# The gate's power on GpSimd for all tiles, and the first tile turned between the matmuls of the third output projection

## The chip, the cores and the metric

The kernel runs on one core of a Trainium2 chip. Its engines work side by side and meet only at semaphores: TensorE (PE in the profile) multiplies matrices, VectorE (DVE) and ScalarE (ACT) work on rows, GpSimd (POOL) takes elementwise work on data in SBUF, and SyncE (SP) issues transfers. The metric is the device time of one execution in microseconds; less is better.

## The reference

One layer of a small transformer in float32, over 4 batches of 256 tokens of width 512 (1024 tokens, 8 tiles of 128):

```
x = x + layernorm(attention(layernorm(x)))        # 32 heads of 16, 8 key/value heads, rotary, causal
x = x + layernorm(ffn(layernorm(x)))
ffn(x):  result = x @ W_base.T + b_base
         probs = softmax(x @ W_gate.T)            # 8 experts
         top two, renormalised: route_w
         delta = sum over experts of (x @ A.T * route_w) @ B.T
         return result + delta
```

Renormalising the top two of a softmax needs only the difference of their two logits: with l1 the largest and l2 the second, the second weight over the first is e^(l2 - l1), and the weights are 1/(1 + that) and that/(1 + that). This one number per token is "the gate's power" of the title.

## The kernel before, in words

The program is written out by hand, one instruction stream per engine; there is no scheduler. Each `wait_ge` is a wait on a semaphore, and each engine works strictly in the order of its stream. After the projections, attention runs over 32 units in a software pipeline of `STEPS` steps. Behind it comes the part that the change touches: a pipeline over the 8 tiles of 128 tokens, `tile_step(s)`, which each engine has in a form of its own. In step s tile s is in the output projection, tile s-1 gets its first residual and the norm ahead of the feed-forward part, tile s-2 is transposed and multiplied with the concatenated weights (base, down projection, gate), tile s-3 is gated and goes through the up projection, tile s-4 gets bias and statistics, and tile s-5 its last norm and residual. Steps 0 and 1 are interleaved with the end of attention (`EARLY`), steps 2 to 12 follow it.

What each engine does in step s, in its order:

- TensorE: `turn_mid(s-2)` (L1188, four transposes), `project_out(s)` (L1179, 12 matmuls: four with the high parts of weight and attention, four with the low part of the weight, four with the low part of attention), `base_down_router(s-2)` in three terms (L1204, 8 matmuls each), with `turn_hw(s-3)` (L1215, one transpose of the gated down projection) behind the first term, and `up_projection(s-3)` (L1219, L1221). Step 2 alone is the other way round: `project_out(2)` first, then waits for the last exponentials and the last copies of attention's output, then `turn_mid(0)`.
- ScalarE: in steps 3 and 4 the gate's power (L678: Exp with scale -1 and the largest logit as bias) and then a one-element square root that brings that function's table back (`bring_table(1, ..)`, L582); `high_of_transpose(s-2)` (L664); square roots of variances (L588); the first residual's norm (L651); the copy of the turned gated tile (L697). At the end of steps 2 and 3 a one-element Exp brings the exponential's table. `attn_high_part` (L658) follows steps 2 and 4.
- VectorE: `gating_choice(s-3)` (L881 the eight largest logits, L883 their indices, L884, L885 the one-hot of the first), `add_bias(s-4)` (L912, L913), statistics of tile s-1 (L777, L778), `gating_weights(s-3)` (L892, L893, L896, L897 make the weights from the power; L901 multiplies the down projection with them), statistics of the output projection of tile s (L777), the low part of the transposed tile s-2 (L937), and the scales and norms (L783, L786, L791).
- GpSimd: from step 5 on `gate_power(s-3)`, then the last residual of tile s-5 (L531) and the first residual of tile s (L536). `attn_low_part` (L513) stands at the end of step 2 and inside step 5, `divide(3)` (L507) at the end of step 3. `gate_power` is a subtraction and a power, both of 128 x 1:

```
pool.wait_ge(top_ready, t + 1)
pool.tensor_tensor(ga[:, 18:19], ga[:, 9:10], ga[:, 8:9], ALU.subtract).then_inc(logit_left, 1)
pool.wait_ge(logit_left, t - POWER_TILE + 1)
pool.tensor_tensor(ga[:, 1:2], e_sb[:, :], ga[:, 18:19], ALU.pow).then_inc(gexp_ready, 1)
```

VectorE's L892 waits for `gexp_ready`. TensorE's `turn_hw` waits for `hw_ready`, which L901 gives; its first term of tile t waits for `xn1_high` (L664) and, from tile 2 on, for `y_ready` of tile t-2 (L913).

Of the kernel before, what the change touches and what calls it, by code (L numbers as in the profile page):

```python
# [65 lines left out]

VECTOR_ATTN = {UNITS: 0, UNITS + 4: 1}
SPREADS = {21: (0,), 25: (1,), UNITS + 1: (2, 3), 37: (4,), 41: (5,), 45: (6,), 49: (7,)}
POWER_TILE = 2


ROPE_3 = {0: 1, 1: 2}
# [11 lines left out]
def build(nc, x, wq, wk, wv, wo, wcat, lora_b, bias, tables, ident, maskq, iota, out):  # L84
    ctx = ExitStack()
    with ctx:
# [360 lines left out]
        def _(pool):  # L447
# [68 lines left out]
            def gate_power(t):  # L516

                ga = gate[:, t % 2, :]
                pool.wait_ge(top_ready, t + 1)
                pool.tensor_tensor(ga[:, 18:19], ga[:, 9:10], ga[:, 8:9], ALU.subtract).then_inc(logit_left, 1)  # L520
                pool.wait_ge(logit_left, t - POWER_TILE + 1)
                pool.tensor_tensor(ga[:, 1:2], e_sb[:, :], ga[:, 18:19], ALU.pow).then_inc(gexp_ready, 1)

            def residuals(s):
# [35 lines left out]
                    pool.tensor_tensor(low, whole, high.bitcast(F32), ALU.subtract).then_inc(weight_low, 1)  # L560
            divide(BATCH - 2)
            for s in range(2, TILES + 5):
                if POWER_TILE <= s - 3 < TILES - 1:
                    gate_power(s - 3)
                if s == TILES + 1:
                    gate_power(TILES - 1)
                if s == 5:
                    attn_low_part(BATCH - 1)
                residuals(s)
                if s == 3:  # L570
                    divide(BATCH - 1)
                if s == 2:
                    attn_low_part(BATCH - 2)
# [3 lines left out]
        def _(act):  # L577
            act.wait_ge(pool_const, 1)

            def bring_table(k, t):  # L580

                nc.scalar.activation(unused[:, k, t:t + 1], eps_sb[:, 0:1], (ACT.Exp, ACT.Sqrt)[k])  # L582
# [90 lines left out]

            def tile_step(s):
                t1, t2, t3, t4, t5 = (s - lag for lag in range(1, 6))
                if 0 <= t3 < POWER_TILE:
                    act.wait_ge(top_ready, t3 + 1)
                    nc.scalar.activation(gate[:, t3 % 2, 1:2], gate[:, t3 % 2, 8:9], ACT.Exp, scale=-1.0,  # L678
                                         bias=gate[:, t3 % 2, 9:10]).then_inc(gexp_ready, 1)
                    bring_table(1, t3)  # L680
                if 0 <= t2 < TILES:
                    high_of_transpose(t2)
                if s < TILES:
# [15 lines left out]
                    output_norm(t5)  # L699
                if 0 <= t4 < TILES:  # L700
                    sqrt(3, t4)
                if 0 <= t2 < POWER_TILE:
                    bring_table(0, t2)

            for n in range(STEPS):
                u = n - ST_LAG
# [302 lines left out]
        def _(pe):  # L1009
# [150 lines left out]
                if kt == qt:  # L1160
                    last.then_inc(o_psum, 1)

            def project_out(t):
                if t == 0:

                    pe.wait_ge(weight_low, 8)
                    pe.wait_ge(s12_free, UNITS)
                if t == 1:

                    pe.wait_ge(mrow_ready, GROUPS)  # L1170
                pe.wait_ge(attn_low, t // 2 + 1)
                if t >= 2:
                    pe.wait_ge(z1_ready, t - 1)
                b = t // 2
                terms = [(attn, w, r) for attn, w in ((attn_h[:, b % 2, :], wo_h), (attn_h[:, b % 2, :], wo_l),
                                                      (attn_l[:, b, :], wo_h)) for r in range(REP)]
                for i, (attn, w, r) in enumerate(terms):
                    col = r * SEQ + (t % 2) * P
                    last = nc.tensor.matmul(ps[:, (t + 1) % 2, :], attn[:, col:col + P], w[:, r, :],  # L1179
                                            start=(i == 0), stop=(i == len(terms) - 1))  # L1180
                last.then_inc(wo_psum, 1)

            def turn_mid(t):
                pe.wait_ge(xn1_ready, t + 1)
# [39 lines left out]
            def tile_step(s):  # L1224
                t2, t3 = s - 2, s - 3
                if s == 2:

                    project_out(s)

                    pe.wait_ge(exp_done, 2 * UNITS)  # L1230
                    wait_o(pe, 2 * GROUPS)
                if 0 <= t2 < TILES:
                    turn_mid(t2)
                if 3 <= s < TILES:
                    project_out(s)
# [83 lines left out]
```

## Time and profile before

| | |
|---|---|
| median of 3 runs | 234.10 us (232.86 to 234.14) |
| the profiled execution's own time | 233.25 us |
| its span, first to last instruction | 231.5 us |
| PE busy | 202.0 us (87%) |
| DVE busy | 173.6 us (75%) |
| ACT busy | 116.8 us (50%) |
| POOL busy | 115.4 us (50%) |
| granted TensorE clock, mean | 0.991 of full speed |

A busy share is an average over the whole span. What a change in one stage is worth is read from that stage: which engine waits there, and what ends its wait last. The tile pipeline's steps 2 to 12 fill the stretch from about 159 us to the end.

### The profile page before, as it was taken

The page shows a single profiled execution, that of the slowest core. Times are in us where ns is not written, and L with a number is a line of the kernel's source. Part 1 is how long each engine was busy: PE and PEld are TensorE (multiplying, and loading weights), DVE is VectorE, ACT ScalarE, POOL GpSimd, SP SyncE. Part 2 cuts the span into 40 slices and gives each one's busy share as a digit, 9 for nine tenths or more (in the row PEclk, how much of TensorE's full clock was granted, in tenths as well). Part 3 has the DMA queues.
Part 4 walks back from the last instruction along what each step waited for, and adds up shares of the span by engine and source line. Part 5 has one row for each costly group of instructions (what it writes and reads, how often), then busy time and mean ns, then how long its engine had stood idle before and what let it go on. Part 6 is the DMA issues. An engine that isn't in the chain of part 4 may idle for free.

```text
span 231.5 us, 3767 instructions
## 1 busy us (share of the span) xinstructions
PE 202.0 (87%) x1304; PEld 122.8 (53%) x1304; DVE 173.6 (75%) x364; ACT 116.8 (50%) x207; POOL 115.4 (50%) x102
## 2 busy tenths in 40 slices
PE   0599999998878979999999989899889989997860
PEld 0484834444444444444444424145778878996840
DVE  1882616867998896859696885685898898898885
ACT  3340531243124877878766785773578335343231
POOL 8200333553357795797743446462756275323352
PEclk9999999999999999999999999999999999999996
DMA  5998049977985102795762203354230000110113
GB/s 166 381 363 338 3 136 204 256 201 167 193 206 144 38 1 72 185 193 103 171 118 65 49 11 51 96 96 96 47 98 0 3 19 26 47 48 0 45 45 136
DMA packets 22465, 26.73 MB, mean 115 GB/s; under 512 B 3760, under 2 KB 17328, under 8 KB 21680
## 3 DMA queue, kind: packets, MB, share of 16 engines
q1 hardware_dynamic: 22304, 26.38, 44.8%
q8 instruction: 10, 0.16, 0.3%
q10 hardware_dynamic: 144, 0.13, 0.2%
q14 instruction: 7, 0.06, 0.1%
HBM read 17.19 MB, written 6.95 MB: 104 GB/s over the span
## 4 chain that ended last, share of the span: by engine, by line
PE 44%; DVE 29%; issue 9%; ACT 8%; DMA 5%; SPq 3%; POOL 1%; DVEq 0%; ACTq 0%; POOLq 0%
PE ps L1046 10%; DVE stats L777 5%; PE ps L1141 5%; PE ps L1156 5%; PE ps L1056 4%; PE ps L1204 4%; DVE nmax L977 3%; PE ps L1115 3%; PE ps L1032 3%; DMA region_b<-q_scr 3%; DVE nmax L974 2%; PE ps L1095 2%; ACT region_a L724 2%; PE ps L1110 2%; DMA x_sb<-x 2%
## 5 line engine op out<-in xcount | busy, mean ns | idle before, releaser
L544 POOL TENSOR_SCALAR_AFFINE_SELECT region_a<-region_a 128x1024 f32<-128x1024 f32 x32 | 36.9, 1153 | 27.4 <-ACT region_a L724 27.1
L977 DVE TENSOR_REDUCE nmax<-ps 128x4 f32<-128x1024 f32 x32 | 39.1, 1222 | 10.3 <-PE ps L1115 10.0
L724 ACT ACTIVATE region_a<-ps 128x1024 f32<-128x1024 f32 x32 | 32.7, 1022 | 0.2 <-PE ps L1141 0.2
L1046 PE MATMUL ps<-region_a,region_c 128*128 128x512 f32 x64 | 29.0, 598 | 0.0
L1141 PE MATMUL ps<-region_b,kst 98*128 98x512 bf16 x96 | 26.9, 381 | 1.6 <-ACT region_a L724 1.1
L721 ACT ACTIVATE region_a<-ps 128x512 f32<-128x512 f32 x32 | 19.2, 599 | 16.9 <-PE ps L1141 16.2
L974 DVE TENSOR_REDUCE nmax<-ps 128x4 f32<-128x512 f32 x32 | 21.8, 682 | 5.1 <-PE ps L1099 4.7
L1156 PE MATMUL ps<-region_a,v_aug 128*32 128x512 f32 x192 | 25.3, 603 | 0.0
L588 ACT ACTIVATE std<-mv,eps_sb 128x1 f32<-128x1 f32 x32 | 9.4, 294 | 29.7 <-DVE mv L778 29.7
L536 POOL TENSOR_TENSOR x_sb<-x_sb,region_b 128x512 f32<-128x512 f32 x8 | 10.2, 1276 | 24.8 <-ACT region_b L651 24.8
L463 POOL TENSOR_TENSOR region_a<-region_a 128x512 f32<-128x512 f32 x4 | 6.5, 1627 | 27.6 <-DVE region_a L825 27.6
L1115 PEld LDWEIGHTS ps<-kst,region_b 96*128 96x128 bf16 x256 | 17.0, 97 | 5.5
L1115 PE MATMUL ps<-kst,region_b 96*128 96x128 bf16 x256 | 19.5, 219 | 0.0
L1046 PEld LDWEIGHTS ps<-region_a,region_c 128*128 128x128 f32 x64 | 11.6, 190 | 12.8 <-issue 12.8
L825 DVE TENSOR_TENSOR region_a<-ps,region_c 128x512 f32<-128x512 f32 x16 | 9.9, 683 | 10.3 <-PE ps L1032 5.5
L1095 PE MATMUL ps<-mask_bf,ident_bf 128*128 128x512 bf16 x32 | 12.3, 385 | 4.2 <-DVE nmax L974 2.1
L777 DVE BATCH_NORM_STATS2 stats<-x_sb 128x6 f32<-128x512 f32 x16 | 11.0, 686 | 6.6 <-DMA x_sb<-x 5.6
L1110 PE MATMUL ps<-mask_bf,ident_bf 128*128 128x512 bf16 x32 | 12.3, 385 | 2.6 <-DVE nmax L977 2.4
L1204 PE MATMUL ps<-wcat_h,xn_h 128*128 128x324 f32 x64 | 11.6, 321 | 3.0 <-ACT xn_h L664 1.9
L1141 PEld LDWEIGHTS ps<-region_b,kst 98*128 98x128 bf16 x96 | 7.6, 97 | 12.3 <-ACT region_a L724 3.4
L611 ACT CAST region_c<-region_a 128x512 bf16<-128x512 f32 x8 | 4.7, 618 | 18.1 <-DVE region_a L833 17.1
L531 POOL TENSOR_TENSOR region_b<-x_sb,region_b 128x512 f32<-128x512 f32 x7 | 9.0, 1280 | 8.9 <-ACT region_b L651 8.8
(107 smaller groups left out, 413.9 us busy)
## 6 DMA issues: line engine op xcount, KB each, us to landing
q_scr<-region_c SPq DMA_DIRECT2D x24, 128.0 KB, 2.6
region_b<-q_scr SPq DMA_DIRECT2D x8, 384.0 KB, 4.9
x_sb<-x SPq DMA_DIRECT2D x8, 256.0 KB, 5.8
region_b<-q_scr SPq DMA_DIRECT2D x8, 256.0 KB, 5.6
attn_t<-o_sb SPq DMA_DIRECT2D x32, 64.0 KB, 2.3
rden_bc<-r_scr SPq DMA_DIRECT2D x8, 256.0 KB, 3.4
out<-region_b SPq DMA_DIRECT2D x7, 256.0 KB, 2.0
kst<-k_scr SPq DMA_DIRECT2D x8, 192.0 KB, 3.1
```

What stands on the lines that cost most here:

```text
L544: pool.affine_select(out=blocks, in_=blocks, compare_op=ALU.is_ge, fill=0.0, base=0, pattern=[[0, 2], [0, REP], [1, P]], channel_multiplie ...
L721: nc.scalar.activation(probs[:, u % PRING, 0, :], ps[:, 3, :], ACT.Exp, scale=float(HEAD_DIM) ** -0.5).then_inc(exp_done, 1)
L724: nc.scalar.activation(probs[:, u % PRING, 1:3, :], ps[:, 4:6, :], ACT.Exp, scale=float(HEAD_DIM) ** -0.5).then_inc(exp_done, 1)
L777: link(nc.vector.bn_stats(stats[:, k, t, :], src))
L974: nc.vector.tensor_reduce(nmax[:, gi % 2, 0, heads], ps[:, 0, :].rearrange("p (r k) -> p r k", r=REP), AX.X, ALU.max, negate=True).then_in ...
L977: nc.vector.tensor_reduce(nmax[:, gi % 2, 1, heads], ps[:, 1:3, :].rearrange("p a (r k) -> p r a k", r=REP), AX.XY, ALU.max, negate=True). ...
L1046: last = nc.tensor.matmul(ps[:, SET_BANKS[i][ri], :], wq_sb[:, c, col:col + P], xn_t[:, c, half * HALF:(half + 1) * HALF], start=(c == 0), ...
L1095: nc.tensor.matmul(ps[:, 0, :], ident_bf[:, :], mask_bf[:, :, :].rearrange("p r k -> p (r k)"), start=True, stop=False, skip_group_check=True)
L1115: last = nc.tensor.matmul(ps[:, 1 + kt, r * P:(r + 1) * P], qst[0:SROWS, slot, h, P:2 * P], kst[0:SROWS, slot, k, kt * P:(kt + 1) * P], st ...
L1141: last = nc.tensor.matmul(ps[:, 3 + j, :], kst[0:TROWS, slot, k, kt * P:(kt + 1) * P], qst[0:TROWS, slot, k * REP:(k + 1) * REP, qt * P:(q ...
L1156: last = nc.tensor.matmul(ps[32 * j:32 * j + 32, 6 + qt, :], v_aug[:, 2 * b + kt, g * GROUP_KV + j, :], probs[:, u % PRING, qt + kt, :], s ...
L1204: last = nc.tensor.matmul(ps[:, 4 + 2 * (t % 2) + hf, 0:CATH], act_part[:, t % 2, c, :], w[:, c, hf * CATH:(hf + 1) * CATH], start=(term = ...
```

## The change

`POWER_TILE` is gone. GpSimd takes the gate's power for tiles 0 and 1 too: `gate_power(0)` stands behind `residuals(2)` and ahead of `attn_low_part(2)`, `gate_power(1)` behind `residuals(3)` and ahead of `divide(3)`. ScalarE loses its two exponentials of the gate and the four one-element activations, with the four loads of a table that they cause. On TensorE `project_out(2)` is cut in two: its first 8 matmuls, then `turn_mid(0)`, then its last 4, and only then the waits for the last exponentials and copies.

```diff
--- before.py
+++ after.py
@@ -66,7 +66,6 @@
 
 VECTOR_ATTN = {UNITS: 0, UNITS + 4: 1}
 SPREADS = {21: (0,), 25: (1,), UNITS + 1: (2, 3), 37: (4,), 41: (5,), 45: (6,), 49: (7,)}
-POWER_TILE = 2
 
 
 ROPE_3 = {0: 1, 1: 2}
@@ -518,7 +517,7 @@
                 ga = gate[:, t % 2, :]
                 pool.wait_ge(top_ready, t + 1)
                 pool.tensor_tensor(ga[:, 18:19], ga[:, 9:10], ga[:, 8:9], ALU.subtract).then_inc(logit_left, 1)
-                pool.wait_ge(logit_left, t - POWER_TILE + 1)
+                pool.wait_ge(logit_left, t + 1)
                 pool.tensor_tensor(ga[:, 1:2], e_sb[:, :], ga[:, 18:19], ALU.pow).then_inc(gexp_ready, 1)
 
             def residuals(s):
@@ -560,13 +559,15 @@
                     pool.tensor_tensor(low, whole, high.bitcast(F32), ALU.subtract).then_inc(weight_low, 1)
             divide(BATCH - 2)
             for s in range(2, TILES + 5):
-                if POWER_TILE <= s - 3 < TILES - 1:
+                if 2 <= s - 3 < TILES - 1:
                     gate_power(s - 3)
                 if s == TILES + 1:
                     gate_power(TILES - 1)
                 if s == 5:
                     attn_low_part(BATCH - 1)
                 residuals(s)
+                if s in (2, 3):
+                    gate_power(s - 2)
                 if s == 3:
                     divide(BATCH - 1)
                 if s == 2:
@@ -673,11 +674,6 @@
 
             def tile_step(s):
                 t1, t2, t3, t4, t5 = (s - lag for lag in range(1, 6))
-                if 0 <= t3 < POWER_TILE:
-                    act.wait_ge(top_ready, t3 + 1)
-                    nc.scalar.activation(gate[:, t3 % 2, 1:2], gate[:, t3 % 2, 8:9], ACT.Exp, scale=-1.0,
-                                         bias=gate[:, t3 % 2, 9:10]).then_inc(gexp_ready, 1)
-                    bring_table(1, t3)
                 if 0 <= t2 < TILES:
                     high_of_transpose(t2)
                 if s < TILES:
@@ -699,8 +695,6 @@
                     output_norm(t5)
                 if 0 <= t4 < TILES:
                     sqrt(3, t4)
-                if 0 <= t2 < POWER_TILE:
-                    bring_table(0, t2)
 
             for n in range(STEPS):
                 u = n - ST_LAG
@@ -1160,7 +1154,7 @@
                 if kt == qt:
                     last.then_inc(o_psum, 1)
 
-            def project_out(t):
+            def project_out(t, first=0, end=3 * REP):
                 if t == 0:
 
                     pe.wait_ge(weight_low, 8)
@@ -1174,11 +1168,13 @@
                 b = t // 2
                 terms = [(attn, w, r) for attn, w in ((attn_h[:, b % 2, :], wo_h), (attn_h[:, b % 2, :], wo_l),
                                                       (attn_l[:, b, :], wo_h)) for r in range(REP)]
-                for i, (attn, w, r) in enumerate(terms):
+                for i in range(first, end):
+                    attn, w, r = terms[i]
                     col = r * SEQ + (t % 2) * P
                     last = nc.tensor.matmul(ps[:, (t + 1) % 2, :], attn[:, col:col + P], w[:, r, :],
                                             start=(i == 0), stop=(i == len(terms) - 1))
-                last.then_inc(wo_psum, 1)
+                if end == len(terms):
+                    last.then_inc(wo_psum, 1)
 
             def turn_mid(t):
                 pe.wait_ge(xn1_ready, t + 1)
@@ -1225,11 +1221,13 @@
                 t2, t3 = s - 2, s - 3
                 if s == 2:
 
-                    project_out(s)
+                    project_out(s, 0, 2 * REP)
+                    turn_mid(t2)
+                    project_out(s, 2 * REP)
 
                     pe.wait_ge(exp_done, 2 * UNITS)
                     wait_o(pe, 2 * GROUPS)
-                if 0 <= t2 < TILES:
+                elif t2 < TILES:
                     turn_mid(t2)
                 if 3 <= s < TILES:
                     project_out(s)
```

GpSimd's stream from the residual of step 2 to that of step 4. L536 (first residual), L513 (low part of attention) and L507 (division) of the kernel before are L535, L512 and L506 of the changed one; L519 and L521 are the subtraction and the power. Before:

```order
L536 TENSOR_TENSOR x_sb<-x_sb,region_b 128x512 [waits z1_ready]
L513 TENSOR_TENSOR attn_l<-attn_t,attn_h 128x1024 [waits attn_low,attn_high]
L536 TENSOR_TENSOR x_sb<-x_sb,region_b 128x512 [waits z1_ready]
L507 TENSOR_TENSOR attn_t<-attn_t,rden_bc 128x1024 [waits num_loaded3,rden_loaded3,rden_loaded2,num_loaded2]
L536 TENSOR_TENSOR x_sb<-x_sb,region_b 128x512 [waits z1_ready]
```

After:

```order
L535 TENSOR_TENSOR x_sb<-x_sb,region_b 128x512 [waits z1_ready]
L519 TENSOR_TENSOR gate<-gate 128x1 [waits top_ready]
L521 TENSOR_TENSOR gate<-e_sb,gate 128x1 [waits logit_left]
L512 TENSOR_TENSOR attn_l<-attn_t,attn_h 128x1024 [waits attn_low,attn_high]
L535 TENSOR_TENSOR x_sb<-x_sb,region_b 128x512 [waits z1_ready]
L519 TENSOR_TENSOR gate<-gate 128x1 [waits top_ready]
L521 TENSOR_TENSOR gate<-e_sb,gate 128x1 [waits logit_left]
L506 TENSOR_TENSOR attn_t<-attn_t,rden_bc 128x1024 [waits num_loaded3,rden_loaded3,rden_loaded2,num_loaded2]
L535 TENSOR_TENSOR x_sb<-x_sb,region_b 128x512 [waits z1_ready]
```

Two pairs of small instructions came in, each between a residual and one of the two long instructions over 1024 columns.

TensorE's stream in step 2, from the second four matmuls of the third output projection to the first term of tile 0 (L1179, L1188, L1204 are L1174, L1184, L1200 in the changed kernel). Before:

```order
L1179 MATMUL ps<-wo_l,attn_h 128x512 x4
L1179 MATMUL ps<-wo_h,attn_l 128x512 x4
L1188 MATMUL ps<-ident_sb,region_b 128x128 [waits xn1_ready,o_ready_vector,exp_done]
L1188 MATMUL ps<-ident_sb,region_b 128x128 x3
L1204 MATMUL ps<-wcat_h,xn_h 128x324 [waits xn1_high]
```

After:

```order
L1174 MATMUL ps<-wo_l,attn_h 128x512 x4
L1184 MATMUL ps<-ident_sb,region_b 128x128 [waits xn1_ready]
L1184 MATMUL ps<-ident_sb,region_b 128x128 x3
L1174 MATMUL ps<-wo_h,attn_l 128x512 [waits z1_ready,attn_low]
L1174 MATMUL ps<-wo_h,attn_l 128x512 x3
L1200 MATMUL ps<-wcat_h,xn_h 128x324 [waits xn1_high,o_ready_vector,exp_done]
```

The four transposes moved ahead of the last four matmuls, and the waits for the copies and exponentials moved from the transposes to the first term. The other engines' streams differ only on ScalarE, by the ten instructions named above that are gone.

## Rows read from the trace of the kernel before

**Rows 1.** Busy time of each engine, one stretch per tile step, s = 3, 4, 6 and following
```profile
core 0: us, PE busy (x) PEld busy (x) DVE busy (x) ACT busy (x) POOL busy (x), PEclk, DMA share, GB/s
167.90:176.54 8.64, 8.05 (x48) 6.97 (x46) 7.24 (x23) 6.43 (x12) 4.24 (x3) 1.00 0.25 65
...
176.54:185.01 8.47, 8.28 (x48) 6.91 (x46) 7.83 (x21) 4.53 (x12) 3.52 (x3) 1.00 0.01 2
...
193.88:201.65 7.77, 7.77 (x47) 7.05 (x45) 7.00 (x27) 3.12 (x7) 3.43 (x5) 1.00 0.09 35
```

**Rows 2.** The chain that ended last, in order of time: start us, us, what
```profile
176.67 2.32 DVE gate L885
...
212.33 0.36 DVE region_b L901
```

**Rows 3.** Timeline, step s = 2: start us, us, engine, line, op, operands, [idle before]
```profile
160.58 1.09 PE L1179 MATMUL ps<-wo_l,attn_h 128*128 128x512 f32 x4
...
161.68 0.55 DVE L791 TENSOR_SCALAR region_b<-x_sb,mv,rstd 128x512 f32<-128x512 f32 x1
...
162.93 0.63 PE L1188 MATMUL ps<-ident_sb,region_b 128*128 128x128 f32 x4 [0.33 <-DVE o_sb L286]
...
164.23 1.45 PE L1204 MATMUL ps<-wcat_h,xn_h 128*128 128x324 f32 x8 [0.68 <-ACT xn_h L664]
...
164.66 0.67 DVE L777 BATCH_NORM_STATS2 stats<-ps 128x6 f32<-128x512 f32 x1
```

**Rows 4.** Timeline, step s = 3
```profile
167.27 1.28 POOL L536 TENSOR_TENSOR x_sb<-x_sb,region_b 128x512 f32<-128x512 f32 x1 [1.20 <-ACT region_b L651]
...
168.10 0.17 DVE L881 MAX8 gate<-ps 128x8 f32<-128x8 f32 x1 [0.49 <-PE ps L1204]
...
169.72 2.38 POOL L513 TENSOR_TENSOR attn_l<-attn_t,attn_h 128x1024 fp32r<-128x1024 f32 x1 [1.17 <-ACT attn_h L658]
...
169.86 1.28 ACT L582 ACT_TABLE_LOAD   x1
...
169.94 2.18 DVE L893 TENSOR_SCALAR gate<-iota_sb,gate 128x8 f32<-128x8 f32 x1
...
171.88 1.47 PE L1204 MATMUL ps<-wcat_h,xn_h 128*128 128x324 f32 x8 [0.59 <-ACT xn_h L664]
...
172.43 0.35 DVE L901 SCALAR_TENSOR_TENSOR region_b<-ps,gate 128x128 f32<-128x128 f32 x1
```

**Rows 5.** Timeline, step s = 4
```profile
175.33 1.27 POOL L536 TENSOR_TENSOR x_sb<-x_sb,region_b 128x512 f32<-128x512 f32 x1 [3.23 <-ACT region_b L651]
...
176.36 0.27 DVE L884 CAST gate<-gate_i 128x2 f32<-128x2 uint32 x1
...
176.56 2.40 POOL L507 TENSOR_TENSOR attn_t<-attn_t,rden_bc 128x1024 f32<-128x1024 f32 x1
...
176.67 2.32 DVE L885 TENSOR_SCALAR gate<-iota_sb,gate 128x8 f32<-128x8 f32 x1
...
180.99 0.35 DVE L901 SCALAR_TENSOR_TENSOR region_b<-ps,gate 128x128 f32<-128x128 f32 x1
```

**Rows 6.** Timeline, step s = 5, where GpSimd already takes the power
```profile
185.38 0.19 POOL L520 TENSOR_TENSOR gate<-gate 128x1 f32<-128x1 f32 x1 [0.19 <-DVE gate L881]
...
185.65 0.55 POOL L522 TENSOR_TENSOR gate<-e_sb,gate 128x1 f32<-128x1 f32 x1
...
185.81 0.23 DVE L885 TENSOR_SCALAR gate<-iota_sb,gate 128x8 f32<-128x8 f32 x1
...
186.17 2.40 POOL L513 TENSOR_TENSOR attn_l<-attn_t,attn_h 128x1024 fp32r<-128x1024 f32 x1
...
187.47 1.12 DVE L893 TENSOR_SCALAR gate<-iota_sb,gate 128x8 f32<-128x8 f32 x1
...
188.53 1.28 POOL L531 TENSOR_TENSOR region_b<-x_sb,region_b 128x512 f32<-128x512 f32 x1
```

**Rows 7.** Line L885 over the whole run: shortest, median and longest, first and last start
```profile
L885 DVE TENSOR_SCALAR gate<-iota_sb,gate x8: 229/231/2320, 168.8 to 220.2; 128x8 f32<-128x8 f32 x8
```

## The prediction

> **What bounds the kernel now.** I read the stretch of the tile steps first, one window per step from one turn of a tile to the next [rows 1]. The reader should compare the lengths: steps 3 and 4 take 8.64 and 8.47 us, step 6 takes 7.77 us with as many matmuls, and in step 6 TensorE is busy for all of its 7.77. So an undisturbed step is bound by TensorE (with VectorE at 7.00 us not far behind), and steps 3 and 4 hold 0.87 + 0.70 = 1.57 us above that, which is most of what this change can reach. In both of them VectorE is busier than in step 6 (7.24 and 7.83) although it does no more work: something makes its instructions long.
>
> The chain of waits says where [rows 2]: it runs through VectorE's L885 at 176.67 for the whole of that instruction's 2.32 us, and it is still on VectorE at 212.33. Apart from its waits for ScalarE's small square roots, the chain does not leave VectorE between these two. Hence a time won on VectorE at the end of step 4 moves all that follows, and time won on TensorE or ScalarE alone does not.
>
> The timelines of the steps name the cause. L885 works on 8 columns; its median over the run is 231 ns, its longest 2320 [rows 7]. The long one starts at 176.67, 0.11 us behind the start of GpSimd's division over 1024 columns (L507, 176.56 for 2.40, end 178.96), and ends at 178.99 [rows 5]. In step 3 the same happens to L893, from 169.94 to 172.12, beside L513, which ends at 172.10 [rows 4]. VectorE's small instructions of this kind are held until a long GpSimd instruction ends. The question for each step is thus which VectorE instruction meets the long one of GpSimd, and when that one starts.
>
> **Step 2: the turn moved into the projection.** Before, the second four matmuls end at 160.58 + 1.09 = 161.67, the last four at 162.60; TensorE is idle for 0.33 us until 162.93 (a copy of attention's output) and for another 0.68 between the turn and the first term at 164.23 [rows 3]. Now the turn needs only the norm of L791, which ends at 161.68 + 0.55 = 162.23. TensorE waits from 161.67 to about 162.3, turns for 0.63 until 162.9, and the last four matmuls cover ScalarE's copy of the turned tile and end at 164.0, where the first term starts: 0.2 us earlier than 164.23. The gain is so small because the idle 1.01 us becomes one of 0.63 plus nothing, and the start stamps overlap. What is put late is the third output projection, by 1.4 us (162.60 to 164.0). VectorE asks for it at 164.66 (L777), so 0.66 us of cover stays. Bounds: if the turn began no sooner than before (162.93), the matmuls would end at 162.93 + 0.63 + 1.09 = 164.65, still inside the cover, and the gain would be below zero by 0.4 on TensorE; at best it is the whole idle second. I take 0.2. The other waits moved behind the last matmuls are over by then: the copy that ended the idle 0.33 is done at 162.9.
>
> **Step 3: the power of tile 0.** Removed from ScalarE: two exponentials and four one-element activations, each of these with a table load of 1.28 us ahead of it [rows 4]: some 5 us of loads over both steps. On TensorE they cost what is seen at 171.88, 0.59 us of waiting for the copy of turned tile 1 [rows 4]; now that copy can run as soon as the tile is turned, beside the output projection. TensorE's gain would be 0.2 + 0.59 = 0.8 us there, but the next thing that it needs is `turn_hw(0)`, behind VectorE's L901, so what counts is VectorE.
>
> VectorE: L881 comes 0.2 us earlier, at 167.9, and the largest logits are ready at about 168.05. GpSimd is in L536 until 168.55 [rows 4]. Behind it come the two new instructions. Their price is in step 5: the subtraction starts at 185.38, the power 0.27 later at 185.65 for 0.55, and L513 follows without a gap (0.52 after the power's start) [rows 6]. Together 0.79 us. So the power starts at 168.8, L513 at 168.55 + 0.79 = 169.34 and, after 2.38, it ends at 171.72 instead of 172.10. (It can start then: ScalarE no longer loads a table ahead of the high part that it needs.) L893 needs the power, which is ready just as L513 begins, so it is held again, until 171.72 instead of 172.12. From there to the end of L901 is 172.78 - 172.12 = 0.66 [rows 4]: 172.4 instead of 172.78, a gain of 0.38 us. It carries over to the first residual of tile 3 (L536 at 175.33 becomes 174.95).
>
> **Step 4: the power of tile 1.** Now the two small instructions stand between L536 and the division. L536 ends at 176.60 - 0.38 = 176.22; the division starts 0.79 later, at 177.0, and ends at 179.4 (before 178.96). VectorE gets its logits 0.4 us earlier; L884 (before at 176.36) starts at about 175.95, L885 at about 176.2 to 176.3. That is behind L536 and ahead of the division, with only the subtraction and the power beside it. Does the power hold it? In step 5 L885 ran at 185.81, inside the power of 185.65 to 186.20, in 0.23 us [rows 6], which is the median of its eight executions [rows 7]. So I take 0.23. From L885's start to L893's it took 187.47 - 185.81 = 1.66 us in step 5 [rows 6], with the same instructions between; so L893 asks at 177.9 to 178.0, finds the division running and is held until 179.4. L901 ends 0.66 later, at 180.1, against 180.99 + 0.35 = 181.34 [rows 5]. Gain on VectorE, and so on all that follows: 1.25 us. Bounds of this term: 1.25 + 0.84 where L893 is not held; 0.4 us lost where L885 still is (rivals below). TensorE can follow: at 7.77 a step instead of 8.64 and 8.47 [rows 1] its own gain by the end of step 4 is up to 0.2 + 1.57 = 1.8 us.
>
> **From step 5 on** I cost nothing: GpSimd has the power there already, every engine starts from VectorE's result, and the holds of step 5 (L893 for 1.12, at L513's end [rows 6]) keep their distance. Work of the added instructions on GpSimd itself, 1.5 us, is hidden: it was busy for 4.24 of 8.64 and 3.52 of 8.47 us in these steps [rows 1].
>
> **The sum.** The profiled execution took 233.25 us, a span of 231.5 and 1.75 around it. 233.25 - 1.25 = 232.0 us. That execution lies 0.85 under the median of the runs (234.10), so the same gain seen from the median would be 232.85; the range has to hold that.
>
> **Rivals.**
>
> *GpSimd's row closes (slower).* The new instructions hold L885 as the long ones do, or it comes too late, and the division begins before it got through. For it: each of the three long instructions of GpSimd in steps 3 to 5 catches a small one of VectorE [rows 4 to 6], and L884 at 176.36 took 0.27. Against: L885 beside the power in rows 6, and that a held instruction does get in where two long ones follow each other: L893 ended at 188.59 although L531 had begun at 188.53 [rows 6]. Price: if only tile 1 is caught, L885 ends at 179.4 instead of 178.99, and the time is 233.25 + 0.4 = 233.7. If tile 0's L885 is caught as well, behind L536 and until 171.7, the work behind it up to L901, 1.7 us (from L885's end at 178.99 to 181.34, less 0.66 for a bias that step 3 has not), ends at 173.4 instead of 172.78; this 0.6 is carried to step 4, where L507 again ends 0.8 behind its old distance: about 234.7. It decides from the point where L885 asks later than the power's end, 0.7 us later than I put it in step 4. The Trainium skill has a rule on this side: "GPSIMD Engine Reference", section "Key points", says that GpSimd shares its SBUF interfaces with VectorE and that VectorE's two-port modes and instructions with two SBUF inputs contend with it, without regard to the length of the GpSimd instruction. By that rule L885 would wait for the subtraction and the power as well, and this rival would be the forecast; the trace agrees for the long instructions (2.32 us), and not for the power (0.23 us in it).
>
> *No hold in step 4 (faster).* L893 escapes the division, because that one starts later (its transfers, or ScalarE) or L893 earlier. Then L901 ends at about 179.0 and TensorE becomes the bound: 233.25 - 1.8 = 231.5; with the hold of step 5 (1.12 - 0.28 = 0.84) gone too, 230.6. Against it: the division has 2.4 us and L893 falls into its middle.
>
> *The gain does not reach the end (no change).* VectorE's lead is lost again in steps 5 to 7, where a last residual of GpSimd may catch an instruction that it let pass before; one such hold is worth 0.8 us: 232.8, two of them 233.25 or above. Against it: all engines start step 5 with the same shift.
>
> **How the numbers follow.** Forecast 0.52 (its own range 231.5 to 232.6, from 0.4 us of uncertainty in where the holds end), slower rival 0.15, faster rival 0.15, no change 0.18. A difference of 1% is 2.3 us, about what a measurement of this kernel can tell from none. The forecast, the no-change case and the slower rival at 233.7 are all within it; the faster rival passes it only where both holds go (230.6), and I allow for holds that I did not see: 0.09 for faster. The slower rival at 234.7 stays within 1%; only more holds of that kind would pass it: 0.04. The range takes in the faster rival down to 231.0, the runs' scatter, and the slower rival's first form: 231.0 to 233.9.
>
> **What would show each step right or wrong.** Right: no table load behind 160 us; the first term of tile 0 at about 164.0 with no wait ahead of it; no wait for ScalarE's copy ahead of tile 1's first term; L893 of tile 0 long and ending at about 171.7; L885 of tile 1 at 0.23 and L893 of tile 1 long, ending with the division at about 179.4; steps 3 and 4 near 8.4 and 7.8 us, step 5 as before. Wrong: an L885 of 2 us or more in step 3 or 4 (slower rival), an L893 of 0.28 us in step 4 (faster rival), or a step from 5 on that is longer than its counterpart before (no change). The forecast fails altogether if statistics of tile 2's output projection wait for TensorE, the cover of 0.66 us being gone.

## The result and the profile after

| | before | changed |
|---|---|---|
| median of 20 runs each | 233.62 us | 232.31 us |
| lowest to highest | 232.24 to 234.72 | 230.92 to 233.46 |
| the profiled execution's own time | 233.25 us | 232.62 us |
| its span | 231.5 us | 230.9 us |

The ratio of changed to before is 0.9947, with a 95% interval of 0.993 to 0.9964: 1.2 us faster, clear of no change but under 1%. (With 20 runs of each kernel the interval is about 0.4 us to either side: a difference of 0.5% can be told from none, where the prediction had put the limit at about 1%.) The two profiled executions differ by 0.63 us only. The rest is not the change's: in the changed kernel's profile everything is already 0.61 us late when the stretch in question begins; most of that is there from the start, where the first loads came later (VectorE's statistics of tile 1 wait for their load until 7.03 us, before until 6.50). A fixed distance is therefore used below, from the start of VectorE's norm of tile 0 in step 2 (161.68 before [rows 3], 162.29 now) to the start of tile 7's turn: 54.46 us before, 53.18 after, 1.28 less. Of these, 0.39 us lie before the turn of tile 1, 0.10 in step 3, 0.71 in step 4 and 0.07 in step 5; the first two are best read together (see e1).

The step windows of the changed kernel, as in [rows 1] (now the third to the sixth window, steps 3, 4, 5 and 6):

```profile
core 0: us, PE busy (x) PEld busy (x) DVE busy (x) ACT busy (x) POOL busy (x), PEclk, DMA share, GB/s
168.12:176.66 8.54, 8.17 (x47) 7.02 (x45) 7.46 (x24) 2.74 (x6) 5.24 (x5) 1.00 0.30 71
176.66:184.42 7.76, 7.76 (x48) 7.04 (x46) 7.08 (x22) 2.68 (x7) 4.44 (x5) 1.00 0.01 2
184.42:193.22 8.80, 8.19 (x47) 7.02 (x45) 8.09 (x25) 3.75 (x8) 5.55 (x6) 1.00 0.08 30
193.22:200.98 7.76, 7.76 (x48) 7.03 (x46) 6.98 (x27) 3.12 (x7) 3.42 (x5) 1.00 0.09 35
```

Step 4 fell from 8.47 to 7.76 us, the length of an undisturbed one; TensorE is busy for all of it. Step 3 (8.54, before 8.64) and step 5 (8.80) still hold about 0.8 and 1.0 us above that. ScalarE's busy time fell from 6.43 and 4.53 us to 2.74 and 2.68, far more than the steps did.

The chain that ended last, in order of time (start, duration, what), against [rows 2]:

```profile
170.34 2.04 DVE gate L887
...
178.64 1.39 DVE gate L887
...
186.88 1.05 DVE gate L887
188.03 1.15 DVE gate L891
```

The 2.32 us of L885 in step 4 are gone from it, but VectorE's L887 (the old L893) is on it for 2.04, 1.39 and, in step 5, 1.05 us, and L891 (the old L897) for 1.15.

Step 2 in the timeline, against [rows 3]; L1184 is the turn, L1174 the projection, L1200 the first term:

```profile
162.29 0.55 DVE L785 TENSOR_SCALAR region_b<-x_sb,mv,rstd 128x512 f32<-128x512 f32 x1
...
162.90 0.66 PE L1184 MATMUL ps<-ident_sb,region_b 128*128 128x128 f32 x4 [0.62 <-DVE region_b L785]
...
163.31 1.18 PE L1174 MATMUL ps<-wo_h,attn_l 128*128 128x512 f32 x4
...
164.33 1.44 PE L1200 MATMUL ps<-wcat_h,xn_h 128*128 128x324 f32 x8
...
165.29 0.67 DVE L771 BATCH_NORM_STATS2 stats<-ps 128x6 f32<-128x512 f32 x1
```

From the norm's start the first term now begins after 2.04 us, before after 2.55. VectorE's L771 (old L777) asks for the finished projection at 165.29, 0.80 us behind its end (163.31 + 1.18), and does not wait.

Step 3, against [rows 4]:

```profile
167.91 1.29 POOL L535 TENSOR_TENSOR x_sb<-x_sb,region_b 128x512 f32<-128x512 f32 x1 [1.19 <-ACT region_b L652]
...
168.80 0.43 DVE L878 CAST gate<-gate_i 128x2 f32<-128x2 uint32 x1
...
169.16 0.18 POOL L519 TENSOR_TENSOR gate<-gate 128x1 f32<-128x1 f32 x1
...
169.42 0.55 POOL L521 TENSOR_TENSOR gate<-e_sb,gate 128x1 f32<-128x1 f32 x1
...
169.94 2.39 POOL L512 TENSOR_TENSOR attn_l<-attn_t,attn_h 128x1024 fp32r<-128x1024 f32 x1
...
170.26 2.11 DVE L887 TENSOR_SCALAR gate<-iota_sb,gate 128x8 f32<-128x8 f32 x1
...
171.34 1.36 PE L1200 MATMUL ps<-wcat_h,xn_h 128*128 128x324 f32 x8
...
172.66 0.35 DVE L895 SCALAR_TENSOR_TENSOR region_b<-ps,gate 128x128 f32<-128x128 f32 x1
```

The residual (L535), the subtraction, the power and the low part (L512) follow each other without a gap. L878, 128 x 2, takes 0.43 us instead of 0.17 and ends with the residual. L887 takes 2.11 and ends with the low part, at 172.37 and 172.33. No table load stands there any more, and the first term at 171.34 has no idle time ahead of it.

Step 4, against [rows 5]:

```profile
175.56 1.27 POOL L535 TENSOR_TENSOR x_sb<-x_sb,region_b 128x512 f32<-128x512 f32 x1 [3.23 <-ACT region_b L652]
...
176.45 0.41 DVE L878 CAST gate<-gate_i 128x2 f32<-128x2 uint32 x1
...
176.79 0.19 POOL L519 TENSOR_TENSOR gate<-gate 128x1 f32<-128x1 f32 x1
...
176.90 0.23 DVE L879 TENSOR_SCALAR gate<-iota_sb,gate 128x8 f32<-128x8 f32 x1
...
177.07 0.55 POOL L521 TENSOR_TENSOR gate<-e_sb,gate 128x1 f32<-128x1 f32 x1
...
177.59 2.40 POOL L506 TENSOR_TENSOR attn_t<-attn_t,rden_bc 128x1024 f32<-128x1024 f32 x1
...
178.56 1.46 DVE L887 TENSOR_SCALAR gate<-iota_sb,gate 128x8 f32<-128x8 f32 x1
...
180.31 0.35 DVE L895 SCALAR_TENSOR_TENSOR region_b<-ps,gate 128x128 f32<-128x128 f32 x1
```

Here lies the larger part of the gain: L895 ends 0.38 us earlier than before in step 3, and 1.29 us earlier at the end of this step (both with the late start of 0.61 us taken off). L879 (the old L885) starts at 176.90, beside the subtraction and the power, and takes 0.23 us, where before it took 2.32. The division (L506) comes only at 177.59, and it now holds L887 for its last 1.46 us, until 180.02. That hold costs the step nothing that shows: TensorE is busy for all of its 7.76 us.

The description ahead of the prediction says that the engines meet only at semaphores. These rows show a second meeting place: L887 had what it needed, its neighbour L886 ran in 0.12 us just ahead of it, and it was over only when GpSimd's instruction was.

### The profile page after: what moved, and what is told of

The parts are those of the page before. It is cut to its first block, busy times and chain, and to the rows that moved or that the text cites. A ratio compares the mean times of both kernels' runs of the same rounds, so it can differ in the third digit from the quotient of the medians.

```text
span 230.9 us, 3750 instructions
## 1 busy us (share of the span) xinstructions
PE 200.0 (87%) x1292; PEld 123.3 (53%) x1304; DVE 173.0 (75%) x364; ACT 110.8 (48%) x197; POOL 116.8 (51%) x106
## 4 chain that ended last, share of the span: by engine, by line
PE 51%; DVE 30%; issue 8%; ACT 6%; DMA 2%; POOL 1%; SPq 1%; DVEq 0%; ACTq 0%
PE ps L1040 11%; PE ps L1150 7%; PE ps L1135 6%; DVE stats L771 6%; PE ps L1200 5%; PE ps L1109 4%; PE ps L1050 4%; DVE nmax L971 3%; PE ps L1026 3%; DVE gate L887 3%; DVE nmax L968 2%; ACT region_a L718 2%; DMA x_sb<-x 2%; PE ps L1089 2%; PE ps L1104 2%
## 5 line engine op out<-in xcount | busy, mean ns | idle before, releaser
L535 POOL TENSOR_TENSOR x_sb<-x_sb,region_b 128x512 f32<-128x512 f32 x8 | 10.2, 1280 | 23.1 <-ACT region_b L652 23.1
L1109 PE MATMUL ps<-kst,region_b 96*128 96x128 bf16 x256 | 19.6, 219 | 1.4 <-DVE nmax L971 0.8
L771 DVE BATCH_NORM_STATS2 stats<-x_sb 128x6 f32<-128x512 f32 x16 | 11.0, 687 | 7.2 <-DMA x_sb<-x 6.1
L1011 PE MATMUL ps<-ident_sb,region_b 128*128 128x128 f32 x32 | 6.1, 331 | 9.0 <-DVE region_b L785 9.0
L1093 PE MATMUL ps<-kst,region_b 96*128 96x128 bf16 x128 | 12.4, 219 | 1.7 <-ACT mrow L725 0.8
L1089 PEld LDWEIGHTS ps<-mask_bf,ident_bf 128*128 128x128 bf16 x32 | 3.1, 96 | 18.8 <-issue 12.2
```

What stands on the lines that cost most here:

```text
L771: link(nc.vector.bn_stats(stats[:, k, t, :], src))
L1093: last = nc.tensor.matmul(ps[:, 0, r * P:(r + 1) * P], qst[0:SROWS, slot, h, 0:P], kst[0:SROWS, slot, k, 0:P], start=False, stop=(r == REP ...
L1109: last = nc.tensor.matmul(ps[:, 1 + kt, r * P:(r + 1) * P], qst[0:SROWS, slot, h, P:2 * P], kst[0:SROWS, slot, k, kt * P:(kt + 1) * P], st ...
```

## The experiments

Each was compared with runs of the kernel before on the same chip. "Distance" is the one defined above, from the profiled execution.
The intervals are some 0.5 us wide to either side. They tell e4 and e5 from the changed kernel (e7 and e8 hardly), but not e1, e3 or e6; the readings of those three rest on the distance, of one execution each. It repeats well where the kernels should agree: 53.18, 53.18 and 53.20 us for the changed kernel, e1 and e9, 54.46 and 54.49 for the kernel before and e2.

| kernel | ratio to before, 95% interval | distance, us | against before |
|---|---|---|---|
| before | 1 | 54.46 | |
| changed | 0.9947 (0.993 to 0.9964) | 53.18 | -1.28 |
| e1 power only | 0.996 (0.994 to 0.998) | 53.18 | -1.28 |
| e2 turn only | 0.9996 (0.9974 to 1.0018) | 54.49 | +0.03 |
| e3 power behind division | 0.9974 (0.995 to 0.9998) | 54.11 | -0.35 |
| e4 three waits | 0.9894 (0.9867 to 0.9922) | 51.83 | -2.63 |
| e5 operands in PSUM | 0.9848 (0.9823 to 0.9874) | 50.94 | -3.52 |
| e6 tables back | 0.9972 (0.9949 to 0.9994) | 53.36 | -1.10 |
| e7 three waits, turn behind | 0.9914 (0.9896 to 0.9933) | 52.27 | -2.19 |
| e8 one wait | 0.991 (0.9888 to 0.9932) | 52.17 | -2.29 |
| e9 strided | one run | 53.20 | -1.26 |
| e10 operands in PSUM, turn behind | one run | 51.39 | -3.07 |

Theory: VectorE's small instructions are held by GpSimd's long ones, and the gain is that the two new GpSimd instructions stand where L885 of tile 1 comes through. Rivals: TensorE's idle time in step 2 was won; or ScalarE's table loads were the cost.

**e1 and e2: each half alone.** e1 takes the turn back:

```diff
-                    project_out(s, 0, 2 * REP)
-                    turn_mid(t2)
-                    project_out(s, 2 * REP)
+                    project_out(s)
...
-                elif t2 < TILES:
+                if 0 <= t2 < TILES:
                     turn_mid(t2)
```

> The changed kernel with its turn of tile 0 put back behind the whole third output projection; the power stays on GpSimd. Theory (the gain comes from where GpSimd's long instructions meet VectorE's small ones): the first power still starts when the residual of step 2 ends, so VectorE's steps 3 and 4 are those of the changed kernel and the time is within 0.2 us of it, 1.1 to 1.3 us (0.5%) under the kernel before. Rival (TensorE's idle time in step 2 is what was won): only about 0.2 to 0.6 us under the kernel before.

e2 is the kernel before with those lines the other way round.

> The kernel before with only the turn of tile 0 moved into the third output projection; ScalarE keeps the power of tiles 0 and 1. Theory: TensorE's first term starts some 0.2 us earlier, but VectorE's one-hot of tile 1 is still held by the division for 2.3 us; time within 0.2 us of the kernel before. Rival: 0.6 us or more under it.

Measured: e1 is as fast as the changed kernel (the same distance, 53.18), e2 as slow as the kernel before (54.49). What e1 keeps, the power on GpSimd with the table loads gone, is worth all of the gain, and the turn's place none: from the norm to the turn of tile 1 e1 takes 6.27 us (changed 5.83), and step 3 then 8.08 (changed 8.54). In e1 the turned tile's logits come later, but GpSimd's row still begins when the residual of step 2 ends, so L887 asks later and is held for 1.89 us instead of 2.11, to the same end:

```profile
169.96 2.40 POOL L512 TENSOR_TENSOR attn_l<-attn_t,attn_h 128x1024 fp32r<-128x1024 f32 x1
...
170.49 1.89 DVE L887 TENSOR_SCALAR gate<-iota_sb,gate 128x8 f32<-128x8 f32 x1
```

**e3: the same work on GpSimd in the other order.**

```diff
-                if s in (2, 3):
+                if s == 2:
                     gate_power(s - 2)
                 if s == 3:
                     divide(BATCH - 1)
+                    gate_power(s - 2)
```

> The changed kernel with the power of tile 1 behind the division of step 3 instead of ahead of it. Theory: the division follows the residual without a gap and holds VectorE's one-hot of tile 1 again (about 2.3 us); the tile's weights are then made without a hold. Only the 0.4 us of step 3 stay: 0.4 us under the kernel before (ratio 0.998). Rival (what counts is that ScalarE's table loads are gone): still 1.2 us under it.

The timeline of e3, step 4 (L880 is the old L885, L888 the old L893):

```profile
177.31 2.38 POOL L506 TENSOR_TENSOR attn_t<-attn_t,rden_bc 128x1024 f32<-128x1024 f32 x1
...
177.41 2.32 DVE L880 TENSOR_SCALAR gate<-iota_sb,gate 128x8 f32<-128x8 f32 x1
...
181.15 0.28 DVE L888 TENSOR_SCALAR gate<-iota_sb,gate 128x8 f32<-128x8 f32 x1
```

L880 starts 0.10 us behind the division and takes 2.32 us again; 0.35 us of gain stay (the interval of its ratio reaches from 0.995 to 0.9998). No table was loaded by ScalarE in e3, and the power was on GpSimd, yet 0.93 of the 1.28 us are gone: that part of the gain is the order. The 0.35 that stay are step 3's, and they have another source. Before, GpSimd's low part stood idle for 1.17 us for ScalarE's high part (L658) [rows 4], which itself came behind a table load (167.21 to 168.49). The low part started 8.04 us behind the norm of tile 0; in e3 it started 7.66 behind it and in the changed kernel 7.65. That these 0.4 us come from the missing table load, e6 shows below.

**e6: the table loads alone.**

```diff
+                if 0 <= t3 < 2:
+                    bring_table(1, t3)
...
+                if 0 <= t2 < 2:
+                    bring_table(0, t2)
```

> The changed kernel with the four one-element activations, and so the four table loads of 1.28 us, put back on ScalarE where they stood (the power stays on GpSimd). Theory: TensorE waits again some 0.6 us for the turned tile 1 in step 3, but VectorE's holds set the end; the high part of attention comes later, so GpSimd's low part starts 0.4 us later than in the changed kernel and the hold of L887 ends 0.4 later: 0.4 us over the changed kernel, unless L887 gets in just ahead of it (it asks within 0.1 us of that start), then up to 0.2 us under it. Rival (the table loads were the cost): 1.0 us or more over the changed kernel, as slow as the kernel before.

Step 3 of e6 (L891 and L895 are the old L893 and L897):

```profile
168.80 0.28 DVE L891 TENSOR_SCALAR gate<-iota_sb,gate 128x8 f32<-128x8 f32 x1
...
168.91 2.40 POOL L512 TENSOR_TENSOR attn_l<-attn_t,attn_h 128x1024 fp32r<-128x1024 f32 x1 [0.39 <-ACT attn_h L659]
...
169.19 2.14 DVE L895 TENSOR_TENSOR gate<-gate 128x8 f32<-128x8 f32 x1
...
170.88 1.47 PE L1204 MATMUL ps<-wcat_h,xn_h 128*128 128x324 f32 x8 [0.83 <-ACT xn_h L665]
```

L891 did get in, 0.11 us ahead of the low part. But it was not a gain: the next instruction that can be held, L895, was, for 2.14 us. That I had not put into the expectation, which gave up to 0.2 us under the changed kernel for this case. The distance is 0.18 us longer than in the changed kernel, and TensorE waits 0.83 us for ScalarE's copy. The low part did start 0.42 us later again, 8.07 us behind the norm, as before; some 0.25 of that came back because only L899, the weighting of the down projection, was left to do behind the hold. So the four loads, 5.1 us on ScalarE, cost 0.2 us here, and the rival of 1.0 us or more is out by the distance. The medians alone would not tell: 0.9972 with its interval fits 0.2 us over the changed kernel as well as 1.0.

**e4 and e8: GpSimd lets VectorE go first.** e4 adds waits for `hw_ready` ahead of the three long instructions and moves the low part of step 5 behind the last residual; e8 has the wait of step 2 alone.

```diff
                 if s in (2, 3):
                     gate_power(s - 2)
+                    pool.wait_ge(hw_ready, s - 1)
...
-                if s == 5:
-                    attn_low_part(BATCH - 1)
...
+                if s == 5:
+                    pool.wait_ge(hw_ready, 3)
+                    attn_low_part(BATCH - 1)
                 if s < TILES:
```

> The changed kernel, with GpSimd waiting for hw_ready (VectorE's weights of the tile are made) ahead of each of its three long instructions of steps 2, 3 and 5, and the one of step 5 behind the last residual of tile 0. Theory: VectorE's L887 of tiles 0 and 1 takes 0.28 us instead of 2.1 and 1.5, and TensorE becomes the bound: steps 3 and 5 fall from 8.5 and 8.8 us to about 7.8, time 1.7 us under the changed kernel and 2.9 under the kernel before (ratio 0.987). Rival (VectorE's holds are beside the path): within 0.3 us of the changed kernel.

> The changed kernel with a single wait for hw_ready on GpSimd, ahead of the low part of step 2 alone. Theory: only L887 of tile 0 loses its hold of 2.1 us; step 3 falls from 8.5 to about 7.8 us, tile 1 is still held by the division and step 5 stays at 8.8: 0.8 us under the changed kernel, about half of what the three waits give. Rival (one hold removed is made up by the next): within 0.2 us of the changed kernel.

e4's timeline, steps 3 and 5 (L889, L893 and L782 are the old L893, L897 and L786):

```profile
170.18 0.28 DVE L889 TENSOR_SCALAR gate<-iota_sb,gate 128x8 f32<-128x8 f32 x1
...
171.19 2.40 POOL L512 TENSOR_TENSOR attn_l<-attn_t,attn_h 128x1024 fp32r<-128x1024 f32 x1 [1.29 <-DVE region_b L897]
...
185.58 1.29 POOL L530 TENSOR_TENSOR region_b<-x_sb,region_b 128x512 f32<-128x512 f32 x1 [1.42 <-ACT region_b L654]
...
185.83 1.06 DVE L893 TENSOR_TENSOR gate<-gate 128x8 f32<-128x8 f32 x1
...
187.36 2.40 POOL L512 TENSOR_TENSOR attn_l<-attn_t,attn_h 128x1024 fp32r<-128x1024 f32 x1 [0.49 <-DVE region_b L897]
...
188.79 0.98 DVE L782 SCALAR_TENSOR_TENSOR nmr<-mv,rstd 128x1 f32<-128x1 f32 x1
```

In step 3 L889 takes 0.28 us, and the low part starts behind the weights, at 171.19. Steps 3 and 4 are 7.76 and 7.77 us. In step 5 two others are held: L893 by the last residual (1.06) and L782 by the low part (0.98), and the step takes 8.20. The distance is 1.35 us under the changed kernel where I expected 1.7; the shortfall is in step 5. e8's single wait gives 1.01 of it (expected 0.8, and half of what the three give), with step 3 at 7.77 and step 5 at 8.54. In e8 the division still holds L889, tile 1's, for 1.41 us, and step 4 still takes 7.78 us. A GpSimd engine that waits, and is idle for 1.3 us more, makes the kernel faster.

**e5: take VectorE off the way.** Here GpSimd's order is that of the changed kernel. The one-hot of the first expert (L879 of the changed kernel) reads its input in PSUM, in unused columns of the bank that holds the tile's logits; L887 reads and writes there; L891 reads one of its two inputs there. The copies into PSUM are made once, ahead of step 2, with waits that guard them and are not all shown.

```diff
+            for bank in (5, 7):
+                last = nc.vector.tensor_copy(ps[:, bank, 400:408], iota_sb[:, :])
...
-                nc.vector.tensor_scalar(ga[:, 24:32], iota_sb[:, :], ga[:, 16:17], None, ALU.is_equal)\
+                nc.vector.tensor_scalar(ga[:, 24:32], ps[:, 5 + 2 * (t % 2), 400:408], ga[:, 16:17], None, ALU.is_equal)\
...
-                      nc.vector.tensor_scalar(ga[:, 32:40], iota_sb[:, :], ga[:, 17:18], ga[:, 1:2],
+                      nc.vector.tensor_scalar(ps[:, 5 + 2 * (t % 2), 416:424], ps[:, 5 + 2 * (t % 2), 400:408], ga[:, 17:18], ga[:, 1:2],
...
-                      nc.vector.tensor_tensor(ga[:, 40:48], ga[:, 24:32], ga[:, 32:40], ALU.add))
+                      nc.vector.tensor_tensor(ga[:, 40:48], ga[:, 24:32], ps[:, 5 + 2 * (t % 2), 416:424], ALU.add))
```

> The changed kernel with one operand of VectorE's small gate instructions in PSUM instead of SBUF: the numbers of the experts are copied there once, L879 and L887 read them there, L887 writes its result there and L891 reads it there. GpSimd's order is untouched, and its long instructions run at the same places. Theory (VectorE is held because it and GpSimd want the same way into SBUF, and the add of the bias, which has one operand in PSUM, was never held): none of the three is held any more, steps 3 and 5 fall to about 7.8 us, time 1.7 us under the changed kernel (ratio to before about 0.987), whatever GpSimd does. Rival (VectorE's semaphores or order are what waits, not the port): the instructions stay long and the time stays within 0.3 us of the changed kernel.

Step 3 of e5 (L879, L888 and L892 are the old L884, L893 and L897), and its step windows:

```profile
168.67 0.42 DVE L879 CAST gate<-gate_i 128x2 f32<-128x2 uint32 x1
...
169.81 2.40 POOL L513 TENSOR_TENSOR attn_l<-attn_t,attn_h 128x1024 fp32r<-128x1024 f32 x1
...
170.12 0.29 DVE L888 TENSOR_SCALAR ps<-ps,gate 128x8 f32<-128x8 f32 x1
...
170.52 0.14 DVE L892 TENSOR_TENSOR gate<-gate,ps 128x8 f32<-128x8 f32 x1
```

```profile
core 0: us, PE busy (x) PEld busy (x) DVE busy (x) ACT busy (x) POOL busy (x), PEclk, DMA share, GB/s
167.99:175.74 7.75, 7.75 (x47) 7.03 (x45) 5.68 (x24) 2.74 (x6) 5.75 (x7) 1.00 0.32 78
175.74:183.51 7.77, 7.77 (x47) 7.06 (x45) 6.28 (x24) 3.18 (x7) 4.27 (x4) 1.00 0.01 2
183.51:191.29 7.78, 7.78 (x48) 7.06 (x45) 6.41 (x25) 3.28 (x8) 5.64 (x5) 1.00 0.09 34
```

L888 and L892 run inside GpSimd's L513 (169.81 to 172.21) in 0.29 and 0.14 us, and so they do beside the division and the L513 of step 5. The one-hot (L880 here) took 0.23 us each time but met no long instruction in this run, so its form is not tested. The conversion (L879 here, L878 in the changed kernel), still from SBUF to SBUF, is held by the residual as before (0.42 us). All steps shown take 7.75 to 7.78 us, and TensorE has no idle time in any of them. The ratio is 0.9848 (the medians, 230.01 and 233.07 us, give 0.9869): the fastest version here, 3.5 us under the kernel before by the distance. It was 2.24 us under the changed kernel where I expected 1.7. Steps 3 and 5 gave 0.79 and 1.02, as expected; the surplus is the stretch from tile 6's turn to tile 7's, which fell from 6.72 to 6.25 us. There the first term waits in the changed kernel for VectorE's addition of the bias, and in e5 only for ScalarE's copy:

```profile
210.46 1.42 PE L1200 MATMUL ps<-wcat_h,xn_h 128*128 128x324 f32 x8 [1.11 <-DVE region_b L907]
```

```profile
208.11 1.45 PE L1209 MATMUL ps<-wcat_h,xn_h 128*128 128x324 f32 x8 [0.68 <-ACT xn_h L666]
```

The likely reason is that VectorE was held in steps 6 and 7 too, by the last residuals: L887 takes 0.87 and 0.98 us there in the changed kernel and in e4, where that wait is 1.12, and 0.28 in e5. No run takes away those two holds alone.

**e7 and e10: the turn's place, without the holds.** e7 is e4 and e10 is e5, each with the turn put back as in e1.

> The kernel with GpSimd's three waits for hw_ready (experiment e4), with the turn of tile 0 put back behind the third output projection. Theory: without VectorE's holds TensorE bounds steps 3 to 5, so the turn's place counts here where it did not before: 0.2 to 0.4 us over e4. Rival (the turn's place is worth nothing anywhere): within 0.1 us of e4 in the trace's step 3.

> Experiment e5 (operands in PSUM, no holds) with the turn of tile 0 put back behind the third output projection. From the norm of tile 0 in step 2 to the turn of tile 7, e4 took 51.83 us and e7, the same with the turn behind, 52.27. Theory (with the holds gone TensorE bounds every step, so its waits in step 2 count): e5's 50.94 becomes about 51.4. Rival (the difference of e4 and e7 came from something else): 50.9 to 51.0.

The distances are 52.27 against 51.83 and 51.39 against 50.94: 0.44 (a little over the 0.2 to 0.4 expected) and 0.45 us. So the turn's place is worth 0.45 us as soon as TensorE is the bound, and nothing in the change as it was made. (The intervals of e4's and e7's ratios overlap, and e10 is one run, so this rests on the traces.)

**e9: is it a fast mode?**

```diff
-nc.vector.tensor_scalar(ga[:, 32:40], iota_sb[:, :], ga[:, 17:18], ga[:, 1:2],
+nc.vector.tensor_scalar(ga[:, 48:64:2], iota_sb[:, :], ga[:, 17:18], ga[:, 1:2],
```

> The changed kernel with VectorE's L887 writing its 8 numbers to every second column of a stretch of 16 in SBUF, and L891 reading them there; all operands stay in SBUF. It asks why L887 is held. If the hold hangs on a fast mode that the instruction can take only on neighbouring columns, L887 takes some 0.3 us beside a long GpSimd instruction and L891, with two operands in SBUF, is held in its place, so the time is that of the changed kernel within 0.2 us. If any instruction of VectorE with its operands in SBUF is held, L887 still takes 2.1 and 1.5 us for tiles 0 and 1.

```profile
169.43 2.39 POOL L512 TENSOR_TENSOR attn_l<-attn_t,attn_h 128x1024 fp32r<-128x1024 f32 x1
...
169.74 2.11 DVE L887 TENSOR_SCALAR gate<-iota_sb,gate 128x8 f32<-128x8 f32 x1
```

L887 was held for 2.11 and 1.46 us as in the changed kernel, so writing to neighbouring columns is not what makes the hold. Only its writes were strided; its reads were still of neighbouring columns. And since e5 moved both its input and its output, no run says whether reading or writing SBUF is what gets L887 held.

## Why the prediction was right

It gave 232.0 us from 233.25, a gain of 1.25 us; measured are a ratio of 0.9947 (1.24 us of 233.6) and 1.28 us by the distance. Its steps in turn, with the profile's late start of 0.61 us taken off:

- *Step 3, VectorE 0.38 us earlier, still held.* L895 ended at 173.01 - 0.61 = 172.40, as predicted. L512 ended at 172.33 - 0.61 = 171.72, as worked out; the two new instructions had the spacing taken from step 5 (0.26 and 0.52 us). Right.
- *Step 4, L885 runs beside the power.* It started at 176.29 and took 0.23 us; the division ended at 179.38 (predicted 179.4), L895 at 180.05 (180.1). Right, and e3 shows that this is 0.93 us of the gain: with the division first, L880 took 2.32 us.
- *The next hold.* That L893 would fall into the division was predicted, and it was held for 1.46 us. For its like in step 3 e8 shows a worth of 1.0 us. In step 4 it showed no cost, since TensorE was busy throughout, there and in e8. So if L893 had escaped in step 4, as the faster rival supposes, that step had nothing left to give; what was left to win lay in steps 3 and 5.
- *Step 2, 0.2 us.* This term was mis-sized: the first term came 2.55 - 2.04 = 0.51 us earlier. I had added the listed durations of the turn and of the last four matmuls (0.63 and 1.09), while from start to start they take 0.41 and 1.02. It did not reach the sum, since I had counted only what VectorE gains; e1 and e2 confirm that its worth here is zero, and e7 and e10 that it is 0.45 where TensorE is the bound.
- *From step 5 on, nothing.* Step 5 took 8.80 us against 8.87, step 6 7.76 against 7.77. Right. The reading of step 6 as undisturbed was right only of TensorE: a last residual holds L893 there as well, and VectorE's 7.00 us, called "not far behind", are 6.40 in e5.
- *The rivals.* GpSimd's row did not close on VectorE: L878 was held by the residual each time (0.43 and 0.41 us), and L879 still came through. The rule of the Trainium skill weighed there ("GPSIMD Engine Reference", "Key points") does not speak of the GpSimd instruction's length. Here the small ones held nothing visibly. For the long ones, e4, e5 and the changed kernel agree with the rule on instructions with two SBUF inputs (L891: 1.14 us beside the residual of step 5, 0.14 with one input in PSUM); whether L887, with one, is held for a two-port mode no run shows. The faster rival's ceiling for no hold in steps 3 to 5 was a gain of 2.65 us (230.6), and e5 gained 3.52 by the distance. The ceiling had left out the hold of L897 in step 5 (188.71, for 1.12 us in the trace before), half of what step 2 gives, and the stretch behind tile 6's turn.
- *Luck.* Little of it: VectorE's terms, which make the sum, came out one by one within 0.1 us, and step 2's did not enter it. Step 3 as a whole took 8.54 us where I had put it near 8.4. The start of L885 in step 4 came out as predicted although L884 asked 0.1 us sooner than thought, because the residual held it (0.41 us) to its end.

## What to carry to other kernels

Where GpSimd and VectorE both work in SBUF, look in the timeline for small VectorE instructions that end with a long GpSimd one: a 0.28 us instruction that is held for 2 us can stall the whole chain, though the page counts it as busy. Whether it does is read from the step: in step 3 it cost 1.0 us, in step 4 nothing that showed. Moving operands of the held instructions to PSUM removed every long hold here; letting GpSimd wait until the short chain is through removed most; reordering GpSimd, which the change did, removed one and left its successor. And a table load or an idle gap on an engine that is not the bound may be left alone: 5.1 us of loads cost 0.2 us, by the later start of GpSimd's low part.

## What the runs showed of the hardware that I had not expected

- Avoiding a hold for one instruction passes it on to the next of its kind: in e6 L891 came 0.11 us ahead of L512, and L895 behind it took 2.14 us.
- Not all of VectorE's instructions are held. Beside a long GpSimd instruction, ones of 128 x 1 (the changed kernel's L886, 0.12 us), reciprocals (e4's L779, 0.15 us at 188.61), batch statistics (e4's L773, 0.70 us at 171.45) and adds with an operand in PSUM (the changed kernel's L907, 0.34 us) kept their length; held were a comparison over 8 columns (L887, up to 2.11 us), an add and a scale with two operands in SBUF (the changed kernel's L891, 1.14, and e4's L782, 0.98), and, by the residual, a conversion of 2 columns (L878, 0.43 instead of 0.17).
- GpSimd's own long instructions were not lengthened by any of this: 2.38 to 2.42 us with a held instruction beside them, 2.39 and 2.40 without (e4's division, e5's L513).
